# Scores as 16-bit integers in pairs of keys, in a fused patch-embedding, attention and feed-forward kernel

## What is computed

```python
attn = jnp.einsum('bhqd,bhkd->bhqk', q, k) * sc
attn = fake_quant(attn, s_attn)              # clip(round(x / s), -128, 127) * s
...
def int_log_softmax(attn, scale):
    x_int = attn / scale
    x_int = x_int - jnp.max(x_int, axis=-1, keepdims=True)
    n = 30
    x0_int = jnp.floor(-0.6931 / scale)
    x_int = jnp.maximum(x_int, n * x0_int)
    qq = jnp.floor(x_int / x0_int)
    r = x_int - x0_int * qq
    ...
    exp_int = jnp.maximum(jnp.floor((r * (r + b_int) + c_int) * 2.0 ** (n - qq)), 0.0)
    exp_sum = jnp.sum(exp_int, axis=-1, keepdims=True)
    ratio = jnp.round(exp_sum / jnp.maximum(exp_int, 1.0))
    ...                                      # ratio to a power of two, 0 from 2 ** 16 on
```

## Time and profile before

| | us |
|---|---|
| median of 3 runs (lowest, highest) | 1015.75 (1015.71, 1016.1) |
| span of the profiled execution | 1014.5 |
| DVE busy | 876.0 (86%) |
| PE busy | 880.8 (87%) |
| ACT busy | 779.8 (77%) |
| POOL busy | 266.9 (26%) |

### The profile page before, as it was taken

How to read it: one execution, slowest core, us unless ns; L and a number is a source line. 1 busy time by engine, 2 the same in 40 slices (tenths; PEclk the granted TensorE clock), 3 DMA queues, 4 the chain that set the end, 5 groups by cost and what they waited for, 6 DMA issues and landing times. The chain is left out here.

```text
span 1014.5 us, 18281 instructions
## 1 busy us (share of the span) xinstructions
PE 880.8 (87%) x5594; PEld 539.9 (53%) x5594; DVE 876.0 (86%) x1695; ACT 779.8 (77%) x1529; POOL 266.9 (26%) x248
## 2 busy tenths in 40 slices
PE   3568779999999999999999999999999999885757
PEld 1244436555565656565565656565556556453435
DVE  3964899998999899999999999999999999995960
...
DMA packets 132628, 53.42 MB, mean 53 GB/s; under 512 B 105103, under 2 KB 131413, under 8 KB 132437
## 3 DMA queue, kind: packets, MB, share of 16 engines
...
...
## 5 line engine op out<-in xcount | busy, mean ns | idle before, releaser
L563 POOL TENSOR_TENSOR ee_sb<-ee_sb,rs_sb 128x1020 f32<-128x1020 f32 x64 | 157.2, 2464 | 379.1 <-DVE rs_sb L1059 379.1
L1195 PE MATMUL bank<-hats_sb,ht_sb 127*96 127x400 f32 (+1 forms) x384 | 147.9, 522 | 1.7 <-DVE hats_sb L921 1.7
L1327 PE MATMUL bank<-w_out_sb,ge_sb 128*102 128x192 f32 x768 | 138.8, 331 | 10.9 <-DVE y_sb L1096 6.9
L1327 PEld LDWEIGHTS bank<-w_out_sb,ge_sb 128*102 128x102 f32 x768 | 120.3, 168 | 31.6 <-issue 17.8
L921 DVE TENSOR_TENSOR hats_sb<-hats_sb 126x1600 f32<-126x1600 f32 x64 | 127.2, 1987 | 0.7
L648 ACT ACTIVATE hats_sb<-bank 126x400 f32<-126x400 f32 (+1 forms) x256 | 108.2, 523 | 0.3 <-PE bank L1181 0.3
L727 ACT ACTIVATE a_sb<-scores,sc_sb 128x1020 f16<-128x1020 f32 x64 | 71.1, 1111 | 39.2 <-PE scores L1279 39.2
L1195 PEld LDWEIGHTS bank<-hats_sb,ht_sb 127*96 127x96 f32 (+1 forms) x384 | 58.7, 166 | 72.6 <-issue 69.3
L734 ACT ACTIVATE sq_sb<-rm_sb,sc_sb 128x1020 f32<-128x1020 f16 x64 | 73.5, 1148 | 18.2 <-DVE rm_sb L1031 18.0
L572 POOL TENSOR_TENSOR xshift_sb<-mv_sb,xshift_sb 102x4 f32<-102x4 f32 (+1 forms) x33 | 11.0, 333 | 279.9 <-DVE ve_sb L961 278.5
L1242 PE MATMUL bank<-xt_sb,w_in_sb 128*128 128x408 f32 (+1 forms) x204 | 82.0, 527 | 1.0 <-ACT xt_sb L667 1.0
...
## 6 DMA issues: line engine op xcount, KB each, us to landing
...
q_sb<-qb_sb SPq DMA_DIRECT2D x192, 12.8 KB, 1.9
...
```

The lines of the kernel that those rows point to most:

```text
L563: nc.gpsimd.tensor_tensor(EE[b][:], EE[b][:], RS[b][:].unsqueeze(2).to_broadcast([128, RT, TOK]), ALU.mult).then_inc(scaled_done, 1)
L1195: last = mm(dst, HT[0:rows, t.i, j, :], HATS[t.i][0:rows, 1 + j, :], start=(j == 0 and not odd), stop=(j == NCH - 2 and odd == 1))
L1327: last = mm(bank[t.banks[0]][0:TOK, 0:D], GE[:, f, t.i * TOK:(t.i + 1) * TOK], WOUT[:, f, :], start=(f == 0), stop=(f == FT - 1))
```

## The change

Layout: the 1020 elements of a row of partitions are now ordered (pair of keys, row tile, key in the pair), 51 x 10 x 2, instead of (row tile, key), 10 x 102. So a value per row tile, written twice, is a run of 20 elements that repeats 51 times. PE writes its scores into PSUM in this order inside each bank, ACT interleaves the two banks. PR on ACT reads it back to (row tile, key). Types: `A16`, `MA`, `MB`, `MN`, `MX`, `M16`, `GQ` and `RM` are int16 instead of f16. `A16` is clipped once (new step CLP) ahead of the minimum. DST is a tensor_tensor subtraction into int16 that saturates; a shift `LIFT` put into `MX` makes the saturation do the clip that BND did, and BND is gone. QQ, QQG, REM and EP take constants for the new sign and shift. `MX` and `RS` hold 20 values instead of 10. The setup computes seven [128, 1] constants where it computed two.

```diff
-MAGIC16 = 1536.0
+EVEN_LIFT = 1536.0
+I16_MAX = 32767.0
+KP = TOK // 2
+RB = RT // 2
+PAIRS = 2 * RT
...
+        def by_row(flat):
+            return flat.rearrange("p (k r e) -> p r k e", r=RT, e=2)
+        def over_key_pairs(rows):
+            return rows.rearrange("p r e -> p (r e)").unsqueeze(1).to_broadcast([128, KP, PAIRS])
...
-        A16 = [sb(f"a16_{b}", [128, RT, TOK], f16) for b in range(2)]
-        MA = sb("ma", [128, RT, 52], f16)
-        MB = sb("mb", [128, RT, 26], f16)
+        A16 = [sb(f"a16_{b}", [128, RC], i16) for b in range(2)]
+        MA = sb("ma", [128, 26 * PAIRS], i16)
+        MB = sb("mb", [128, 13 * PAIRS], i16)
...
# pool, NRM
-                nc.gpsimd.tensor_tensor(EE[b][:], EE[b][:], RS[b][:].unsqueeze(2).to_broadcast([128, RT, TOK]),
+                scaled = EE[b][:].rearrange("p (k q) -> p k q", q=PAIRS)
+                nc.gpsimd.tensor_tensor(scaled, scaled, over_key_pairs(RS[b][:]),
                                         ALU.mult).then_inc(scaled_done, 1)
# act, SC and PR
-                nc.scalar.activation(A16[b][:].rearrange("p (j r) k -> p j (r k)", j=2), SCORES[:, :, 0:RC // 2], ACT.Identity,
-                                     scale=sc[:, SCORE:SCORE + 1], bias=MAGIC16).then_inc(a16_done, 1)
+                nc.scalar.activation(A16[b][:].rearrange("p (k j q) -> p j k q", j=2, q=RT),
+                                     SCORES[:, :, 0:RC // 2].rearrange("p j (k q) -> p j k q", q=RT), ACT.Identity,
+                                     scale=sc[:, SCORE:SCORE + 1], bias=EVEN_LIFT).then_inc(a16_done, 1)
...
-                nc.scalar.activation(RR[:], EE[b][:].rearrange("p h k -> p (h k)"), ACT.Exp, scale=-1.0).then_inc(rr_done, 1)
+                nc.scalar.activation(RR[:].rearrange("p (r k e) -> p r k e", k=KP, e=2), by_row(EE[b][:]), ACT.Exp,
+                                     scale=-1.0).then_inc(rr_done, 1)
# dve, the softmax
+            def clip(t):
+                a = A16[t.i % 2][:]
+                dve.wait_ge(a16_done, t.count(1, 1))
+                v.tensor_scalar(a, a, EVEN_LIFT - 127.0, EVEN_LIFT + 128.0, ALU.max, ALU.min).then_inc(clip_done, 1)
...
-                v.tensor_tensor(MA[:], A16[b][:, :, 0:52], A16[b][:, :, TOK - 52:TOK], ALU.min).then_inc(half_done, 1)
+                v.tensor_tensor(MA[:], a[:, 0:26 * PAIRS], a[:, 25 * PAIRS:KP * PAIRS], ALU.min).then_inc(half_done, 1)
...
-                v.tensor_reduce(MN[:], MB[:], AX.X, ALU.min).then_inc(min_done, 1)
+                v.tensor_reduce(MN[:], by_row(MB[:]), AX.XY, ALU.min).then_inc(min_done, 1)
...
-                v.tensor_scalar(MX[t.i % 2][:], MN[:], MAGIC16 + 128.0, MAGIC16 - 127.0, ALU.min, ALU.max).then_inc(mx_done, 1)
+                v.tensor_scalar(MX[t.i % 2][:], MN[:].unsqueeze(2).to_broadcast([128, RT, 2]), col(NLIFT), None,
+                                ALU.add).then_inc(mx_done, 1)
...
-                v.scalar_tensor_tensor(M16[b][:], A16[b][:], MAGIC16 + 128.0, MX[b][:].unsqueeze(2).to_broadcast([128, RT, TOK]),
-                                       ALU.min, ALU.subtract).then_inc(m_done, 1)
+                v.tensor_tensor(M16[b][:].rearrange("p (k q) -> p k q", q=PAIRS), A16[b][:].rearrange("p (k q) -> p k q", q=PAIRS),
+                                over_key_pairs(MX[b][:]),
+                                ALU.subtract).then_inc(m_done, 1)
-            def bound(t):
-                v.tensor_scalar(M16[b][:], M16[b][:], 0.0, sc[:, G30:G30 + 1], ALU.max, ALU.min).then_inc(mc_done, 1)
...
-                v.tensor_scalar(QQ[:], M16[t.i % 2][:].rearrange("p h k -> p (h k)"), sc[:, INVG:INVG + 1],
-                                sc[:, NOFFS:NOFFS + 1], ALU.mult, ALU.add).then_inc(qq_done, 1)
+                v.tensor_scalar(QQ[:], M16[t.i % 2][:], col(NINVG), col(QBASE), ALU.mult, ALU.add).then_inc(qq_done, 1)
...
-                v.tensor_scalar(GQ[:], QQ[:], col(G), None, ALU.mult).then_inc(gq_done, 1)
+                v.tensor_scalar(GQ[:], QQ[:], -127.0, col(G), ALU.add, ALU.mult).then_inc(gq_done, 1)
...
-                v.tensor_reduce(SS[b][:], EE[b][:], AX.X, ALU.add).then_inc(ss_done, 1)
+                v.tensor_reduce(SS[b][:], by_row(EE[b][:]), AX.XY, ALU.add).then_inc(ss_done, 1)
...
-                v.reciprocal(RS[b][:], SS[b][:]).then_inc(rs_done, 1)
+                v.reciprocal(RS[b][:], SS[b][:].unsqueeze(2).to_broadcast([128, RT, 2])).then_inc(rs_done, 1)
# pe, SC
-                    dst = SCORES[:, r // (RT // 2), r % (RT // 2) * TOK:(r % (RT // 2) + 1) * TOK]
+                    dst = SCORES[:, r // RB, 0:KP * RT].rearrange("p (k r e) -> p r k e", r=RB, e=2)[:, r % RB, :, :]
```

More of the change, by code:

```diff
@@ L1111, in _ @@
                                                  for k, f in enumerate((fold_bn2, qkv_integers, qkv_weights, proj_weights))},
-                "QKC": qk_cast, "MAX": row_min, "MXB": quarter_min, "MXC": last_min, "DST": distance,
+                "QKC": qk_cast, "CLP": clip, "MAX": row_min, "MXB": quarter_min, "MXC": last_min, "DST": distance,
                 "LN1": lambda t: moments(t, ST1, MV1, st1_done, mv1_done, xh_done), "LS1": moments_a,
@@ L1116, in _ @@
                 "VE2": second_variance,
-                "BND": bound, "QQ": quotient, "QQG": quotient_g, "EP": power_bits, "REM": remainder, "EXP": exp_int,
+                "QQ": quotient, "QQG": quotient_g, "EP": power_bits, "REM": remainder, "EXP": exp_int,
                 "SUM": exp_sum, "RCP": sum_reciprocal, "PW": widen_ratio, "PR": power_of_two,
```

74 lines of the change are left out of this document (38 added, 36 removed).

## The result

The changed kernel takes 1065.34 us (median of 3 runs, 1058.6 to 1065.67) against 1015.75 before: a ratio of 1.0495, 95% interval 1.046 to 1.0529. The forecast was 1019.6, the range 1004 to 1034. The sign was right; the size was wrong by 46 us.

The account below looks back on a forecast made before the run. The prediction took a ring of PE and ACT waits, with DVE's chain in it, as the bound. Span 1014.5 + 4.2 (13 x 0.32) - 0.3 = 1018.4, plus 1.25 outside, gave 1019.6 us; range 1004 to 1034.

Parts of the forecast that it names:

- DVE's savings: On DVE: cheaper DST and no BND, less CLP, MX and RCP costs: -0.32 us per image, -20 us over 64 images.
- Where the saving goes: DVE's saving turns into waits; CLP before MAX delays REM and PE's transpose load: +0.32 us a period, 13 times, +4.2 us.
- the ring: PE and ACT wait for each other each period, DVE's CLP-to-REM chain delaying both; 1017 to 1023 us, chance 0.50.
- rival 1: PE absorbs the delay, or the scores' arrival is not what DVE meets; 1014 to 1017 us, chance 0.17.
- the slack at the load: At PE's weight load for the transpose: 0.09 us left before a late REM delays PE.
- the sum: Span 1014.5 + 4.2 - 0.3 = 1018.4 us; with 1.25 us outside the span, 1019.6 us.
- POOL: ... so 0.: POOL's scaling with repeated values: 2.19 ns per element in a similar row against 2.42 now, so no added cost.
- Strided reads on ACT: Slower strided reads on ACT or in SUM: 1024 to 1034 us, chance 0.04, counted as 0 in the forecast.
- The terms added: Separate costs and savings were summed along the path: +4.2 us over the periods and -0.3 us at the end.
- Rivals 2 to 4: DVE bound, faster, 995 to 1005 us (0.15); PE scores slowed, 1036 (0.09); int16 tensor_tensor at half speed, 1040 to 1066 (0.05).
- The 1.25 us outside the span: Time outside the profiled span, added to the predicted span of 1018.4 us to give 1019.6 us.

Follow-up runs that it names:

- e23: Changed kernel with POOL's scaling in its old walk and ACT's last exponential reading straight through (values wrong): ratio 1.0051.
- b1: Kernel before with POOL's scaling in the changed kernel's walk and ten more reciprocals (values wrong): ratio 1.0176.
- b2: Kernel before with ACT's last exponential reading pairs 80 B apart (values wrong): ratio 1.0091.
- b4: Kernel before with POOL's new walk, ACT's pair reads and 8 idle matmuls per group of four images: ratio 1.0191.

## Why the prediction was right or wrong

- *DVE's savings.* Right in all but the smallest instruction priced (MX, +0.03 us where +0.09 was taken). The -20 us of DVE work show where POOL's walk is the old one: 846.9 against 876.0 busy in e23, -29. They are 9 larger than summed: BND counts in busy time with its full 483 ns and not with the 0.40 us from start to start (5 us), MX is 4 us cheaper, and MXB, QQ and EXP are a little shorter (33, 24 and 17 ns, 5 us); small growths elsewhere, such as MAX's 15 ns, take back the rest.
- *Where the saving goes* (the ring through CLP, REM and the transposes, +0.32 us a period). The wait is there and it is the clip's: PE's transposes wait 20 times in the changed kernel, 19 in e23, 10 without the clip, as before. Its price is not confirmed. In e23 the load follows the scaling by 0.58 us and its wait grew from 0.34 to 0.62 us, as the working had it, yet the period is 55.70 us against 55.67. So in this execution the delay reached PE and was taken up later in the period; that is rival 1's result by another way than the slack at the load. The execution is one of e23's fastest (1013.7 us, the median of its ten runs is 1018.2, 0.28 us a period more), so it can't rule out the +0.32 in the others. e23's ratio of 1.0051 makes 1015.75 x 1.0051 = 1020.9, next to the 1019.6 of the sum. That may be luck: its ten runs go from 1010 to 1025, two of the slowest three at a clock of 0.933 and 0.935 where the others have 0.950 to 0.959.
- *"POOL: ... so 0."* The failed step. The row it leaned on (2.19 ns per element) was a single instruction of the setup, and it was compared with the old form as if both were ordinary. Measured: 2.84 ns per element (2895 / 1020), +0.43 us per image on POOL, and 35 us of longer DVE instructions, on which ACT's exponential then waits. The working had no term for what a longer POOL instruction does to the DVE instructions beside it. On its own the new walk costs the kernel before 1.8% (b1).
- *"Strided reads on ACT": 0.04 of chance, no term.* Failed as well: +0.20 us per image, 0.9% on its own (b2). The diff has the line and no row had such a read on ACT; still it got neither a price nor a place on the path.
- *The terms added.* Failed as a form. ACT's 0.20 us and POOL's 0.43 us per image, which cost 0.9% and 1.8% alone, cost 3.9% together, and with the clip and the rest of the change 4.95%. The missing mechanism was in no rival: more and longer waits of PE ahead of the sampling matmuls, after which those run at half clock. With the clock held up by idle matmuls the changed kernel loses 2.5% and the two together 1.9%.
- *Rivals 2 to 4.* None happened: scores stayed at 215 ns, the int16 subtraction took REM's 0.69 us; DVE as the bound, faster, never.
- *Small readings.* The 1.25 us outside the span compares the runs' median with the span of another execution. In every run above, time and span of the same execution differ by 2.1 us (1058.6 and 1056.5), so the sum is 0.8 us short by it. And with the wait for the scores, DVE was idle for 1.7 us of a period and not for 1.4.

How the 1.0248 that remains at full clock divides among the links of the ring stays open; so does how much of POOL's part goes by its own delay and how much by the held DVE instructions, which no run takes apart. b4 (no clip, no int16) has 1.0191 of it.
